# Two more lookups by one-hot products in place of gathers, held gathers, and the tail in another order, in a recommendation tower

## The reference

```
e = stack([tbl_f[ids[:, f]] for f in 0..26], axis=1)      # (512, 27, 128)
z = einsum('bnd,bmd->bnm', e, e)[:, i, j]                   # i < j: 351 products
h = concatenate([z, dense_ctx], axis=1)                     # (512, 367)
h = maximum(h @ W_top1 + b_top1, 0)                         # 512 wide
h = maximum(h @ W_top2 + b_top2, 0)                         # 256 wide
y = h @ W_top3                                              # (512, 1)
```

## Time and profile before

| what | value |
| --- | --- |
| median of three executions | 115.36 us |
| the profiled execution, its own time | 116.04 us |
| its span, first to last instruction | 114.2 us |
| TensorE busy | 105.0 us, 92% |
| VectorE busy | 74.6 us, 65% |
| ScalarE busy | 71.4 us, 63% |
| GpSimd busy | 71.1 us, 62% |
| bytes moved | 18.67 MB, mean 163 GB/s |

### The profile page before, as it was taken

The page is one execution under the profiler, slowest core; times in us unless marked ns, Lnnn a source line. Parts: engine busy times, 40 slices in busy tenths (PEclk is TensorE's granted clock), DMA queues, the critical chain, the costliest instruction groups (busy, mean ns, idle before and its releaser), DMA issues.

```text
span 114.2 us, 2467 instructions
## 1 busy us (share of the span) xinstructions
PE 105.0 (92%) x1016; PEld 87.8 (77%) x1016; DVE 74.6 (65%) x67; ACT 71.4 (63%) x100; POOL 71.1 (62%) x79
## 2 busy tenths in 40 slices
PE   4949999999997999998999989968899999998992
PEld 4935788887775878785877779958799987996990
DVE  3099999999999999999999506353513206522030
ACT  5059889999999999999999633562412021601021
POOL 3078788788787887979786877677777700003000
DMA  3994887887888766589941122349684610045000
GB/s 36 264 417 189 205 219 278 220 231 291 160 297 289 178 235 163 230 183 406 348 114 46 46 65 56 115 140 248 129 193 133 129 35 0 6 155 83 6 0 1
DMA packets 15573, 18.67 MB, mean 163 GB/s; under 512 B 9265, under 2 KB 11389, under 8 KB 15434
## 3 DMA queue, kind: packets, MB, share of 16 engines
q1 hardware_dynamic: 11239, 13.21, 39.0%
q0 software_dynamic: 1968, 3.99, 12.1%
q10 hardware_dynamic: 2355, 1.32, 4.8%
HBM read 16.74 MB, written 1.77 MB: 162 GB/s over the span
## 4 chain that ended last, share of the span: by engine, by line
DVE 45%; PE 39%; issue 9%; DMA 4%; ACT 0%; DVEq 0%
DVE hot L444 31%; DVE parts L449 12%; PE psG L340 11%; PE psG L368 7%; PE psH L352 6%; PE psH L384 5%; DMA pick_ids<-in_picked_ids 4%; PE psG L323 4%; PE psT L303 2%; PE psG L384 2%; PE psH L399 1%; DVE gram L457 1%; DVE ET L434 1%; PE psG L399 0%; ACT h L556 0%
## 5 line engine op out<-in xcount | busy, mean ns | idle before, releaser
L282 POOL DMA_INDIRECT rows<-in_tbl,ids_sb x60 | 65.5, 1092 | 20.4 <-issue 16.5
L323 PE MATMUL psG<-hot,parts 128*128 128x512 f32 x216 | 56.9, 416 | 2.8 <-ACT parts L516 1.5
L323 PEld LDWEIGHTS psG<-hot,parts 128*128 128x128 f32 x216 | 40.9, 197 | 15.5 <-DVE hot L444 5.1
L444 DVE TENSOR_TENSOR hot<-pick_ids,psH 128x1536 fp32r<-128x1536 int32 (+1 forms) x24 | 44.2, 1889 | 3.9 <-DMA pick_ids<-in_picked_ids 3.8
L526 ACT ACTIVATE hot<-pick_ids,row_no 128x512 fp32r<-128x512 int32 x30 | 19.8, 726 | 0.0
L449 DVE TENSOR_TENSOR parts<-table,parts 128x1024 fp32r<-128x1024 f32 (+1 forms) x12 | 16.3, 1360 | 0.0
L530 ACT ACTIVATE hot<-hot 128x1024 fp32r<-128x1024 f32 (+1 forms) x12 | 15.3, 1274 | 0.4
L457 DVE COPY gram<-psG 128x432 f32<-128x432 f32 x8 | 7.3, 907 | 12.2 <-PE psG L340 12.2
L340 PE MATMUL psG<-ET 128*52 128x54 f32 x512 | 13.4, 212 | 1.8 <-DVE ET L434 1.4
L340 PEld LDWEIGHTS psG<-ET 128*52 128x52 f32 x512 | 13.0, 127 | 2.7 <-DVE ET L434 2.0
L519 ACT CAST parts<-table 128x1280 fp32r<-128x1280 f32 (+1 forms) x11 | 12.9, 1173 | 0.0
(11 more groups left out here) (33 smaller groups left out, 46.7 us busy)
## 6 DMA issues: line engine op xcount, KB each, us to landing
table<-in_tbl SPq DMA_DIRECT2D x6, 640.0 KB, 4.6
table<-in_tbl SPq DMA_DIRECT2D x6, 512.0 KB, 5.5
pick_ids<-in_picked_ids SPq DMA_DIRECT2D x11, 256.0 KB, 3.8
w_sb<-in_w SPq DMA_DIRECT2D x1, 1024.0 KB, 7.7
rows<-in_tbl,ids_sb POOLq DMA_INDIRECT x60, 4.0
pair_blocks<-gram SPq DMA_DIRECT2D x4, 216.0 KB, 2.4
pair_blocks<-gram ACTq DMA_DIRECT2D x4, 216.0 KB, 3.0
w_sb<-in_w SPq DMA_DIRECT2D x1, 512.0 KB, 9.2
```

Of the source, the lines that this page charges most:

```text
L282: pool.indirect_dma_start(out=rows[:, n % RING, x, :], out_offset=None, in_=gathered_tables[f], in_offset=bass.IndirectOffsetOnAxis(ap=ids ...
L323: last = pe.matmul(psP[:, k % 2, :], parts[:, k % 2, x, c, :], hot[:, k % 2, c, :], start=x == 0 and c == 0, stop=x == 1 and c == CH[k] - 1)
L444: dve.tensor_tensor(hot[:, k % 2, first:end, :], pick_ids[:, k % TABLES, :].unsqueeze(1).to_broadcast(shape), numbers.unsqueeze(2).to_broa ...
```

## The change

1. PICKED is 14: the two largest of the picked tables so far gathered become wide picks, so there are 6 picks of 8 chunks and 8 wide ones. 13 features are gathered, 52 transfers, in quads of 4, 4, 4 and 1.
2. The first pick's ids come in two transfers, and the first equality test in two halves of the samples (`first_hot`). WARM_UP is 14.
3. The scratch write follows the first six quads. From gather 21 on, every fourth gather (eight in all, HELD) waits until VectorE has made the one-hot matrix of a wide pick, and stands behind a scratch write.
4. Thirteen quads in place of nine are transposed behind picks (DUE).
5. The units of all four tiles stand in a row, with a quad between each two, and then the layers of the four tiles. `gram` has four buffers, and the layers of tiles 0 and 2 lie in `psG`, those of 1 and 3 in `psH`.
6. SyncE writes both halves of `gram` and issues all reads, but for two of the last tile, which GpSimd issues. ScalarE issues none.

```diff
-    WARM_UP = 10
+    WARM_UP = 14
...
-    DENSE_FROM = 10
+    SHORT = CH.count(min(CH))
+    HELD = range(21, 21 + 4 * (FP - SHORT), 4)
     RING = 10
-    DUE = [2, 3, 4, 5, 6, 7, 9, 10, 11]
+    DUE = [2, 3, 4, 5, 6, 7, 8, 9, 10, 11, 12, 12, 13]
     DURING_PICKS = len(DUE)
-    BY_CHUNK = (0, T - 1)
-    L1_SIGNALS = [0, N1, N1 + 2, N1 + 4]
-    SP_READS = [(0, 1), (0, 1, 2, 3), (0, 1, 2, 3), (0, 2)]
-    ACT_READS = [(2, 3), (), (), (1,)]
+    BY_CHUNK = (0, 2)
+    L1_SIGNALS = [0, N1, N1 + 2, 2 * N1 + 2]
 
...
-        gram = sb("gram", [P, 2, S, F, GH])
+        gram = sb("gram", [P, 4, S, F, GH])
...
 
-            if t == 0:
+            if t in BY_CHUNK:
                 return psG[:, 0, 0, P * (n + 1):P * (n + 2)]
             return psH[:, n, 2, :] if t == T - 1 else psH[:, 0, 2 + n, :]
 
         def y_psum(t):
 
-            if t == 0:
+            if t in BY_CHUNK:
                 return psG[0:1, 1, 0, P:2 * P]
             return psH[0:1, 0 if t == T - 1 else 1, 3, :]
 
...
-        steps = units(0) + [("write", 0)] + quads(9, 10) + units(1) + [("write", 1)] + quads(10, 12) + [("read", 0)]
-        steps += units(2) + [("write", 2)] + quads(12, 13) + mlp(0) + quads(13, 14)
-        steps += [("layer1", 1), ("layer3", 0), ("layer2", 1), ("layer2_end", 1)] + quads(14, 16) + [("layer3", 1)]
-        steps += units(3) + [("write", 3)]
-        steps += mlp(2) + [("read", T - 1), ("layer3", T - 2), ("chunk", 0), ("chunk", 1), ("chunk", 2),
-                           ("chunk", 3), ("relu1", T - 1), ("layer2", T - 1), ("layer3", T - 1)]
+        steps = units(0) + quads(13, 14) + units(1) + quads(14, 15) + units(2) + quads(15, 16) + units(3)
+        steps += [("layer1", 0), ("layer2", 0), ("layer2_end", 0)]
+        for t in range(1, T - 1):
+            steps += [("layer1", t), ("layer3", t - 1), ("layer2", t), ("layer2_end", t)]
+        steps += [("layer1", T - 1), ("layer3", T - 2), ("layer2", T - 1), ("layer3", T - 1)]
...
-                write_blocks(sp, t, 0)
+                for x in range(S):
+                    write_blocks(sp, t, x)
                 sp.wait_ge(blocks_out[t], 16 * S)
-                for c in SP_READS[t]:
+                for c in range(NC) if t < T - 1 else (0, 2):
                     read_pairs(sp, t, c)
...
+            def write_scratch(pauses):
+                if pauses:
+                    pool.wait_ge(paused, pauses)
+                pool.memset(pause[:, :], 0.0).then_inc(paused, 1)
+                return pauses + 1
+
             pauses = 0
+            number = 0
             for n in range(T * NQ):
                 t, q = divmod(n, NQ)
                 if n >= RING:
                     pool.wait_ge(filled, n - RING + 1)
                 for x, f in enumerate(QUADS[q]):
+                    if number in HELD:
+
+                        pool.wait_ge(hot_ready, 2 * (SHORT + HELD.index(number) + 1))
+                        pauses = write_scratch(pauses)
                     pool.indirect_dma_start(
                         out=rows[:, n % RING, x, :], out_offset=None, in_=gathered_tables[f],
                         in_offset=bass.IndirectOffsetOnAxis(ap=ids_sb[:, t, f:f + 1], axis=0),
                     ).then_inc(gathered[t][q], 16)
-                    if n < DENSE_FROM and x == len(QUADS[q]) - 1:
-                        if pauses:
-                            pool.wait_ge(paused, pauses)
-                        pool.memset(pause[:, :], 0.0).then_inc(paused, 1)
-                        pauses += 1
+                    number += 1
+                    if x == len(QUADS[q]) - 1 and number < HELD[0]:
+                        pauses = write_scratch(pauses)
 
             pool.wait_ge(blocks_out[T - 1], 16 * S)
             read_pairs(pool, T - 1, 3)
+            read_pairs(pool, T - 1, 1)
...
                             pe.wait_ge(high_ready, 1)
+                        if k == 0 and x == 0 and c == 0:
+                            pe.wait_ge(half_hot_ready, 1)
                         if x == 0:
                             own = CH[k] - BY_ACT[k]
...
                 if t > 1:
-                    pe.wait_ge(y_ready, t)
+                    pe.wait_ge(y_ready, t - 1)
...
                 if c == 0:
-                    products = U * (T if t == T - 1 else T - 1)
-                    pe.wait_ge(gram_dve, products)
-                    pe.wait_ge(gram_act, products)
+                    pe.wait_ge(gram_dve, U * T)
+                    pe.wait_ge(gram_act, U * T)
+                if c == 0 and t > 0:
+                    pe.wait_ge(y_ready, t - 1)
...
+            def first_hot():
+                shape = [V, HOT_SPLIT, B // 2]
+                numbers = psN[:, 0, 0:HOT_SPLIT].unsqueeze(2).to_broadcast(shape)
+                dve.wait_ge(first_ids_in, 16)
+                dve.tensor_tensor(hot[:, 0, 0:HOT_SPLIT, 0:B // 2], pick_ids[:, 0, 0:B // 2].unsqueeze(1).to_broadcast(shape),
+                                  numbers, ALU.is_equal).then_inc(half_hot_ready, 1)
+                dve.wait_ge(pick_ids_in[0], 16)
+                dve.tensor_tensor(hot[:, 0, 0:HOT_SPLIT, B // 2:B], pick_ids[:, 0, B // 2:B].unsqueeze(1).to_broadcast(shape),
+                                  numbers, ALU.is_equal).then_inc(hot_ready, 1)
+
...
-                for first, end in ((0, HOT_SPLIT), (HOT_SPLIT, own)):
+                for first, end in ((0, HOT_SPLIT), (HOT_SPLIT, own))[k == 0:]:
...
             def unit_copies(m):
-                if m // U >= 2:
-                    dve.wait_ge(blocks_out[m // U - 2], 16 * S)
                 for h in range(H):
                     dve.wait_ge(multiplied[h], 2 * m + 1)
                 dve.tensor_copy(*unit_views(m, 0)).then_inc(gram_dve, 1)
...
+            first_hot()
             for k in range(FP):
                 make_hot(k)
                 split_low(k)
...
+                if k == 0:
+                    act.wait_ge(first_ids_in, 16)
                 act.wait_ge(pick_ids_in[k], 16)
...
                 act.copy(*unit_views(m, 1)).then_inc(gram_act, 1)
-
-            def write_half(t):
-                act.wait_ge(gram_dve, U * (t + 1))
-                act.wait_ge(gram_act, U * (t + 1))
-                write_blocks(act, t, 1)
-
-            def read_half(t):
-                act.wait_ge(blocks_out[t], 16 * S)
-                for c in ACT_READS[t]:
-                    read_pairs(act, t, c)
 
...
-            act.dma_start(pick_ids[:, 0, :], picked_ids[0].partition_broadcast(V)).then_inc(pick_ids_in[0], 16)
+            act.dma_start(pick_ids[:, 0, 0:B // 2], picked_ids[0, 0:B // 2].partition_broadcast(V)).then_inc(first_ids_in, 16)
+            act.dma_start(pick_ids[:, 0, B // 2:B], picked_ids[0, B // 2:B].partition_broadcast(V)).then_inc(pick_ids_in[0], 16)
...
-PICKED = 12
+PICKED = 14
```

14 lines of the change are left out of this document (4 added, 10 removed).

## The result

The changed kernel took 125.32 us (median of 124.93, 124.97, 125.67 and 127.33) against 115.4 us; the ratio is 1.0855, with a 95% interval of 1.0826 to 1.0884. All ratios leave out executions more than 1.5% above the fastest of their kernel (here 127.33), the medians do not. The direction was right and the size too small: 122.5 us was forecast and 124.3 was the upper end of the range. The profiled execution took 124.93 us with a span of 123.1 us, where the sum had 121.4.

| us | before | forecast | after |
| --- | --- | --- | --- |
| VectorE's first wide pick | 32.68 | 31.9 | 32.84 |
| end of the last pick | 67.01 | 76.8 | 77.67 |
| from there to the end | 47.2 | 44.6 | 45.4 |
| span | 114.2 | 121.4 | 123.1 |

The account below looks back on a forecast made before the run. VectorE was taken to bound the picks and TensorE the tail. Span 114.2 + 9.8 (picks) - 2.6 (tail) = 121.4, then + 1.84 - 0.68 = 122.5 us; own range 121.7 to 123.3, with two rivals 121.4 to 124.3.

Parts of the forecast that it names:

- the two picks: Picks on VectorE: two more wide picks at a period of 5.26 us each add 10.52 us.
- Bounds: 0 (halves land together) and -0.85; I take -0.8: Front of VectorE: half the first equality test runs while the second half of the ids travels, saving 0.8 us.
- ScalarE's gain: Front: four more dummies raise the clock before TensorE's first pick, so ScalarE's 1.01 us of waiting goes.
- the two chains are 0.15 apart: End of the picks: TensorE could proceed at 73.55 us by VectorE's chain and 73.7 by ScalarE's; last pick ends at 76.8.
- Then the last pair 3.25: Tail on TensorE: the last pair of units in the row of products takes 3.25 us.
- The sum of the tail, 44.6: From the last pick to the end: products, layers and end take 44.6 us against 47.2, a gain of 2.6.
- the 0.68 taken off: End of the sum: the profiled execution before was 0.68 us above its median, so 0.68 is subtracted.
- the second rival: Serial exchange on SyncE stops the layers of tiles 2 and 3 by up to 1 us each: 123.5 to 124.5 us; chance 0.09.
- The held gathers: GpSimd in the picks: gathers waiting for equality tests cost 0, since last rows land well before transposes run short.
- The first rival, the low clock: First pick on TensorE: clock stays low, ScalarE is 0.25 us late, last pick ends at 78.05: 123.8 us; chance 0.18.
- The shared port as a lock on VectorE: Picks: held gathers in flight block eight subtractions by up to 0.94 us each, 7.5 us: 130 us; chance 0.03.
- The fourth rival: Kernel's end is tied to the gathers; eight fewer save 10 us of GpSimd: about 115.2 us or below; chance 0.04.

Follow-up runs that it names:

- e4: Changed kernel with 12 picks and 15 gathered features instead of 14 and 13, two quads between each two pairs of units: 123.56 us, ratio 1.0726.
- e1: Changed kernel with the first ids in one transfer and the first equality test whole: 125.73 us, ratio 1.0769.
- e10: Kernel before with 14 dummies and the first ids and first equality test in halves: 116.17 us, ratio 1.0060.
- e8: Kernel before with 14 warm-up dummies, nothing else changed: 115.27 us, ratio 0.9999.
- e3: Changed kernel with ten warm-up dummies instead of 14: 124.40 us, ratio 1.0788.
- e6: Changed kernel with the first ids and test whole and ten dummies instead of 14: 123.33 us, ratio 1.0710.
- e9: Changed kernel with ten long dummies and four small ones, keeping TensorE's instruction count as with fourteen: 125.95 us, ratio 1.0950.
- e5: Changed kernel with the layers of tiles 0 and 1 ahead of the last pair of units: 132.12 us, no ratio given.
- e2: Changed kernel without the waits of the eight held gathers, scratch writes behind the first ten quads: 125.15 us, ratio 1.0857.
- e13: Changed kernel run once more, unaltered: 125.98 us, ratio 1.0900.
- e12: Kernel before with 14 dummies, ids and tables of the second and third picks issued only after the first ids landed: 115.09 us, ratio 0.9971.

## Why the prediction was too low

*Right: the two picks.* The forecast had +10.52 us from VectorE's period; e4 against the changed kernel gives 10.73, and VectorE's timeline the same period of 5.26. The sign followed from this. The picks are 10.5 us of a loss of 9.9: all the rest of the change gave 0.6 us back, where the forecast had 3.4.

*Wrong: "Bounds: 0 (halves land together) and -0.85; I take -0.8".* The bound of 0 was too tight. I priced the halves as if the second landed no later than the whole had. Over all profiles the test of the second half starts at 6.61 to 7.00 and that of the whole at 4.79 to 5.73, so it is 1 to 2 us later, and VectorE, which has nothing else to do, is held by it. A half has as many packets as the whole (e1), and that is what I left out. The chain of the picks was 0.16 later at the first wide pick instead of 0.8 earlier. Alone on the kernel before (e10) the split costs 0.7 to 0.9 us, and taking it out of the changed kernel (e1) brings 0.85 back. This is 0.87 us of the error, at the end of the last pick.

*Wrong and harmless: ScalarE's gain.* The clock rose before the first pick as expected, but the 1.0 us that ScalarE won was lost again in its waits for picks, which run at VectorE's pace. My "the two chains are 0.15 apart" treated ScalarE's chain as free of VectorE's. e8 shows that the dummies alone bring nothing.

*Wrong: "Then the last pair 3.25".* The term left out a stop in TensorE's own stream. The sum of the tail, 44.6, was 0.8 too low. The last pair of units took 4.22 us instead of 3.25 (+0.97), and the end behind the last layer 3.13 instead of 2.77 (+0.36; the result has landed 2.06 us behind the start of the last layer before and 2.07 us after, so nearly all of it lies in the instructions that close the program); the layers took 0.07 more, and against that, transposes and waits were 0.55 shorter than forecast. e3, e6 and e9 show that the stop of 0.69 us goes and comes with 16 records of TensorE's stream ahead of it, and e5 that it also takes the dense products of the new order. Of the forecast gain of 2.6 us in the tail 1.8 came.

*Missing: the clock behind the products.* In some executions (one of four of the changed kernel, of e2 and of e13, four of six of e1, two of four of e9) the time is about 2 us longer with a granted clock of 0.97 to 0.99. In e1's profile this is a fall to 0.50 over the first layer, 1.6 us; the rest of these executions have no profile. The median over the profiled execution is 0.39 us, and 0.35 of this is the execution of 127.33: without it the median is 124.97, still above the range. The kernel before (0.985), e3 and e6 have executions with such a mean clock too, and most are no slower. What starts a fall just there stays open; the two stops ahead of it are what the order of the change adds, but the changed kernel's profiled execution has both stops and no fall.

*Wrong: the 0.68 taken off.* The profiled execution of before was 0.68 above its median, and I carried that over to the changed kernel. Its first ids had landed late: the test starts at 5.73 there, in e8 at 4.96 and in e1 at 5.18, and spans of before go from 113.2 to 114.4. The changed kernel's profiled execution was at the low end of its own. The 0.8 for the halves leans on the same late row: with ids that land early the whole test starts at 4.96 and the first half at 4.91, so what the halves were to win and what I took off at the end are largely the same time, counted twice. That the late ids made that execution slow is argued from its profile and e8's (0.77 us apart at the test, 0.93 at the end of the last pick); e12's profiled execution, with the earliest test of all, was its longest. The four pieces sum up: 0.87 + 0.86 (tail, with rounding) + 0.68 + 0.39 = 2.8 us, from 122.5 to 125.3.

*The range.* It had 0.8 for the halves and 0.5 for the tail, and nothing for a base that is itself off. Its upper end, 124.3, was also below the 124.5 that the second rival gave.

*The other steps.* The held gathers cost nothing, as forecast, and e2 shows that they bring nothing either. The first rival, the low clock, did not come true either: e3 and e6 have it, and e3 ends its picks 0.58 us later for it. The rival on the serial exchange did not come true in the new order, where the layers wait for no chunk, but e5 shows how near it is in another. The shared port as a lock on VectorE did not either: the subtraction at 63.03 starts on time behind a gather started at 62.88. The Trainium skill, SBUF — State Buffer, section "SBUF: two separate sides", would have had it blocked, if a gather counts there as an instruction of GpSimd that reads SBUF; the trace agrees only in the other direction, with the gather stretched to 1.65 us at 37.35. The fourth rival, that the end hangs on the gathers, was wrong for the changed order with 14 picks and right for the same order with 12 (e4): I had judged it by the order before, in which the transposes had been put late enough.

## What to carry to other kernels

Before an operand's first load is cut in two, ask when the second half lands, and count packets and not bytes: here a half had the 128 packets of the whole, the first half came no earlier and the second 1 to 2 us later, and an engine that has only this to do loses the difference. A step that shortens a chain which is not the longest is worth nothing, so follow each gain to the engine that sets the pace. A forecast from one profiled execution should first ask how it differs from the others: here the first test started 0.77 us later in one profile than in another (before and e8) and the span was 1.0 us longer, and two terms of the sum counted that same time.

## What the runs showed of the hardware

- A load of 256 KB to 128 partitions cut in two halves along the row has 256 packets of 1,024 bytes in place of 128 of 2,048. The halves ended at 4.1 and 6.3 us (changed kernel), 4.4 and 6.5 (e10), the whole at 4.6 (e8), 4.7 (e1) and 5.3 (before, e6).
- A stop of 0.41 to 0.96 us on TensorE without a releaser, at record 1730 in each of the changed kernel (twice), e1, e2 and e9, and gone with 16 records fewer (e3, e6) or with layers ahead of the last products (e5). A gap of 0.14 to 0.28 us stands 256 records earlier in four of the traces (e13, e2, e9, e6). The stop ends 1.33 to 1.50 us behind the end of a 16 KB piece on the instruction queue.
- A granted clock of 0.50 for 3.4 us in the middle of a busy kernel, behind 0.69 and 1.07 us of idle time (e1), priced at 1.6 us when a layer runs in it. Over a pair of units it took 1.56 us (e4), and over the first pick it cost nothing (e9).
- A gather that starts during a subtraction ends 0.81 to 0.84 us behind the subtraction's end, in the traces before, after and of e2, so it is stretched the more the earlier it starts (2.22 us in e2, 1.65 at 37.35, 0.97 when it starts 1.33 us into it). One that starts 0.15 us ahead of it is not stretched (62.88 and 63.03); the subtraction is on time either way.
